# Stores of the routed experts' outputs: issued from GpSimd's queue instead of SyncE's

## What is computed

```python
logits = x @ router_w                                      # 8 experts, top 2 for each node
combine, dispatch = _top2_gating(logits, capacity)
expert_in = jnp.einsum('nec,nh->ech', dispatch, x)         # 196 slots for each expert
hmid = jax.nn.silu(jnp.einsum('ech,ehf->ecf', expert_in, w1) + b1[:, None, :])
expert_out = jnp.einsum('ecf,efh->ech', hmid, w2) + b2[:, None, :]
y = jnp.einsum('nec,ech->nh', combine, expert_out)
shared = jax.nn.silu(x @ sw1 + sb1) @ sw2 + sb2
out = y + SHARED_SCALE * shared
```

## Time and profile before

| | us |
|---|---|
| median of 3 runs | 1102.03 |
| lowest, highest | 1101.57, 1110.56 |
| profiled execution: its time | 1103.43 |
| profiled execution: span of the instructions | 1101.7 |
| routed experts, first turned slots to the last product of `own` | 973 to 1091 |

### The profile page before, as it was taken

How to read it: one execution, slowest core, us unless ns; L and a number is a source line. 1 busy time by engine, 2 the same in 40 slices (tenths; PEclk the granted TensorE clock), 3 DMA queues, 4 the chain that set the end, 5 groups by cost and what they waited for, 6 DMA issues and landing times.

```text
span 1101.7 us, 14500 instructions
## 1 busy us (share of the span) xinstructions
PE 1063.3 (97%) x5385; PEld 888.4 (81%) x5385; DVE 796.7 (72%) x1632; ACT 416.4 (38%) x647; POOL 410.9 (37%) x264
## 2 busy tenths in 40 slices
PE   6999999999999999999999998999979999999995
PEld 4888778778777777889999998877746877978874
DVE  7587779898989897228676766485479738866647
ACT  3432333443434333132323233451442515246752
POOL 4243788788888775042432230000010000310016
PEclk9999999999999999999999999999989999989997
DMA  9898776788887657687767542523242201578757
GB/s 334 315 316 246 168 209 106 182 229 210 204 228 158 163 121 175 76 187 182 194 169 184 133 123 99 210 93 117 66 73 86 83 2 43 226 264 299 253 184 259
DMA packets 91850, 191.92 MB, mean 174 GB/s; under 512 B 29722, under 2 KB 54877, under 8 KB 83323
## 3 DMA queue, kind: packets, MB, share of 16 engines
q1 hardware_dynamic: 38336, 126.11, 35.5%
q0 software_dynamic: 36032, 33.86, 16.8%
q10 hardware_dynamic: 17406, 30.97, 10.1%
HBM read 136.79 MB, written 54.11 MB: 173 GB/s over the span
## 4 chain that ended last, share of the span: by engine, by line
PE 87%; DVE 9%; ACT 2%; DMA 1%; issue 1%; ACTq 0%; POOLq 0%; SPq 0%; DVEq 0%
PE ps L588 69%; PE ps L896 5%; PE ps L933 4%; DVE rl L418 3%; PE ps L860 2%; DVE EQ L1583 1%; PE ps L578 1%; PE ps L911 1%; DVE V L1503 1%; PE ps L944 1%; PE ps L1027 1%; DMA stage<-in_w_rel 1%; PE ps L813 1%; ACT rh L409 1%; ACT He L1111 1%
## 5 line engine op out<-in xcount | busy, mean ns | idle before, releaser
L2225 POOL DMA_INDIRECT adj_scratch<-cnt,idx x164 | 287.0, 1750 | 131.8 <-DVE idx L1591 51.7
L418 DVE TENSOR_TENSOR rl<-stage,rh 128x512 fp32r<-128x512 f32 (+1 forms) x264 | 215.8, 845 | 138.8 <-ACT rh L409 135.3
L409 ACT CAST rh<-stage 128x512 fp32r<-128x512 f32 (+1 forms) x264 | 181.6, 714 | 343.1 <-PE ps L588 259.9
L588 PE MATMUL ps<-rh,xTh 128*125 128x512 f32 x600 | 237.6, 396 | 1.9 <-DVE xTl L1562 1.0
L588 PE MATMUL ps<-rh,xTl 128*125 128x512 f32 x600 | 236.2, 394 | 0.0
L588 PE MATMUL ps<-rl,xTh 128*125 128x512 f32 x600 | 236.1, 393 | 0.0
L588 PE MATMUL ps<-rh,Ar 125*125 125x342 f32 x600 | 190.8, 323 | 4.6 <-issue 3.3
L588 PE MATMUL ps<-rl,Ar 125*125 125x342 f32 x600 | 190.2, 322 | 0.0
L588 PEld LDWEIGHTS ps<-rh,xTh 128*125 128x125 f32 x600 | 111.1, 185 | 31.6 <-ACT He L1111 1.9
L588 PEld LDWEIGHTS ps<-rh,xTl 128*125 128x125 f32 x600 | 111.2, 185 | 28.0
L588 PEld LDWEIGHTS ps<-rl,xTh 128*125 128x125 f32 x600 | 111.2, 185 | 27.0
(11 more groups left out here) (296 smaller groups left out, 1616.8 us busy)
## 6 DMA issues: line engine op xcount, KB each, us to landing
stage<-in_w_rel SPq DMA_DIRECT2D x22, 1024.0 KB, 6.5
stage<-h_scratch SPq DMA_DIRECT2D x24, 855.0 KB, 6.6
stage<-in_w_e SPq DMA_DIRECT2D x16, 1024.0 KB, 5.3
h_scratch<-He ACTq DMA_DIRECT2D x40, 257.0 KB, 8.2
h_scratch<-He ACTq DMA_DIRECT2D x40, 256.0 KB, 4.2
KR<-key_scratch ACTq DMA_DIRECT2D x37, 256.0 KB, 5.1
stage<-in_w_gate SPq DMA_DIRECT2D x8, 1024.0 KB, 6.1
U<-xe_scratch POOLq DMA_DIRECT2D x16, 392.0 KB, 5.7
```

Source lines behind the costliest of these rows:

```text
L409: e.copy(h, s).then_inc(*a_hi.up(*[("hi", t) for t in step(i)]))
L418: e.tensor_tensor(l, s, h.bitcast(F32), ALU.subtract).then_inc(*v_lo.up(*[("lo", t) for t in step(i)]))
L588: ins = e.matmul(ps[0:P, b, 0:width], a, m, start=first and n == 0, stop=last and n == len(parts) - 1, skip_group_check=again)
L2225: e.indirect_dma_start(accd[to], bass.IndirectOffsetOnAxis(ap=idx[:, n:n + 1], axis=0), cnt16[:, n:n + 1], None, compute_op=ALU.add).then_ ...
```

## The change

The loop in SyncE's program no longer has the stores; it only loads the remaining weights, each as soon as its staging buffer is free. GpSimd's program has the stores instead, with the same two waits for each: after the loads of rows for experts 0 to 4 it alternates the stores of expert n with the loads of rows for expert n + 5, and then issues the rest of the stores. Size and number of all transfers stay, as do the semaphores that they count up.

```diff
-            for n in range(7):
-                for j in range(2):
-                    s, (_, row) = (2 * n + j) % 3, xe_row(n, j)
-                    for hf in range(2):
-                        on.wait_ge(*at("eo", n, j, hf))
-                    e.dma_start(eod[row:row + HC, :], EOs[:, s, :]).then_inc(*d_eo[s].up(("eo out", n, j)))
-                for g in range(first("s1", 0) + 9 + 2 * n, first("s1", 0) + 11 + 2 * n):
-                    if g < len(groups):
-                        load(g)
+            for g in range(first("s1", 0) + 9, len(groups)):
+                load(g)
...
-            for n in range(8):
+            def results_out(n):
+                for j in range(2):
+                    s, (_, row) = (2 * n + j) % 3, xe_row(n, j)
+                    for hf in range(2):
+                        on.wait_ge(*at("eo", n, j, hf))
+                    e.dma_start(eod[row:row + HC, :], EOs[:, s, :]).then_inc(*d_eo[s].up(("eo out", n, j)))
+
+            for n in range(5):
                 slots_in(n)
+            for n in range(7):
+                results_out(n)
+                if n + 5 < 8:
+                    slots_in(n + 5)
```

## The result

| | before | after |
|---|---|---|
| median of 20 runs each, us | 1106.77 | 1109.45 |
| lowest, highest | 1100.98, 1111.67 | 1104.88, 1117.43 |
| profiled execution: time | 1103.43 | 1114.99 |
| its span | 1101.7 | 1113.2 |

The ratio is 1.0044, with a 95% interval of 1.0029 to 1.0058: by the ratio the change costs 4.9 us (3.2 to 6.4), by the medians of the table 2.7. Forecast were +0.7 and 1102.7 us, in a range up to 1106. Part of the distance in absolute time isn't the change: the three runs ahead of the forecast had a median of 1102.03, twenty of the same kernel have 1106.77. In the kernel after, lines behind SyncE's changed loop are 7 lower than before (L926 is L933, L1374 is L1381), and in GpSimd's program L2316 and L2320 are the L2312 and L2316 of before.

What follows compares the result with a forecast made beforehand. Products were taken to bound the stage, and the last store's landing and the add chain the end. +0.22 us issue and +0.50 us packets gave +0.7, on the median 1102.03 making 1102.7 us; range 1101.0 to 1106.

Steps and rivals of the forecast that it cites:

- What bounds the kernel: Routed experts' stage: bound by TensorE's products, 12.50 us in 12.50 us, with the DMA engines 90% busy.
- SyncE's part: SyncE's queue loses 14 stores and 28 waits; staging buffers release the loads, so none starts earlier: value 0.
- at the same distances: Sign in the profile after: weight loads on SyncE still released by low parts, with unchanged distances.
- R1: Rival: stores fight weight loads; 2.7 us late costs nothing, beyond 3.6 us TensorE stalls, to 1111 us; chance 0.12.
- The mild form of R1: Weight loads just over the edge, TensorE stalling 1 us in two or three periods: 1105 us; within R1's chance 0.12.
- The last store: Expert 6's second store, issued by GpSimd: +0.22 us to issue, +0.50 us to first packets, sum +0.7 (+0.2 to +1.7).
- GpSimd's start after the eviction: Issue of the last store after its result's eviction: 0.29 us on GpSimd against SyncE's 0.07, so +0.22 us.
- The chain at the end: After 1064: gathers, sums and adds follow each other in order, each 0.7 us later; the end moves by all 0.7.
- R3: Rival: adds shifted over 1.2 us let VectorE's chunk 2 sum go first, giving back 1.2 us; chance 0.02.
- Copies waiting for stores: ScalarE's copy into a result buffer waits for the store three places before: hidden, or 0.4 us at a 5.3 us store.
- loads of rows behind results: GpSimd's loads of rows 5 to 7 behind waits for results of experts 0 to 2: over 4 us spare, value 0.
- R2: Rival: VectorE holds up GpSimd's writing of descriptors for the last store: +1.0 us more, 1103.7 us; chance 0.06.

Runs made afterwards that it cites:

- pool_double: Kernel after with each store of experts 0 to 4 issued twice from GpSimd, once into an unread tensor; ratio 1.0169, median 1124.78 us.
- sp_double: Kernel before with each store of experts 0 to 4 issued twice from SyncE, once into an unread tensor; ratio 1.0063, median 1113.75 us.
- again: The kernel after run once more, unchanged, against the kernel before; ratio 1.0036, median 1109.48 us.
- split kernels: Each expert weight load cut into two DMAs, applied to before (ratio 0.9995, 1104.97 us) and to after (1.0003, 1106.31 us).

## Why the prediction was wrong

**What bounds the kernel: wrong, though the rows were read right.** "The stage that the change touches is bound by products" held in the one profiled execution. In two others of the same kernel it was bound by the loop of weight loads for stretches. One profile could not show that.

**SyncE's part: right.** Loads are still released by low parts (VectorE's end at 1013.21 + 1.91 = 1015.12, the load at 1015.20), and none comes earlier for lack of stores ahead of it. My sign "at the same distances" did not hold: in after the loads of this buffer are 13.4 and 16.3 us apart (1001.81, 1015.20, 1031.48).

**R1, the slack: here is the step that failed.** I gave the stores against the weight loads 0.12 and set the edge at "3.6 us of room. So 2.7 us late costs nothing". I had followed a late landing once forward, to the slots' low parts and TensorE. That room exists, but as a reserve that is used up: lateness also goes backward, from the low parts to the next load's issue, and comes around again. The edge of a repeated lateness is the loop's, 7.1 us for a load. Before, the loads into this buffer issued at 1012.27 and 1024.50 took:

```profile
stage<-in_w_e SPq DMA_DIRECT2D x1, 1024.0 KB, 6.5
...
stage<-in_w_e SPq DMA_DIRECT2D x1, 1024.0 KB, 8.1
```

The second was already over the edge and the first had 0.6 us to it, not 3.6; and the reserve made up for it. All numbers for that were at hand: that load landed at 1024.50 + 8.1 = 1032.6, the next one into the buffer was issued at 1037.74, 5.1 us later, and 12.25 us is the period. The lateness was mis-sized as well. I added 2.7 us to a load of 5.5, which was one into the other buffer; the loads of the loop became 8.3, 11.2 and 9.9 us, up to 4.7 us more than the 6.5 of before. The mild form of R1, at 1105, was the right mechanism with too small a weight. What the gaps cost through the clock, most of 3.6 us in after, stood in none of my sums.

The Trainium skill, DMA: Bandwidth & Descriptors, "Queues, rings and completion order", says that each DMA engine takes turns between the queues that have work. The 11.7 us between `pool_double` and `sp_double`, with the same bytes, agree with it; that a load in line is served ahead of the stores behind it is my reading and not shown, since I didn't follow single packets. The Trainium skill, DMA: Bandwidth & Descriptors, "Issuing engine by pattern", which sends simple stores to SyncE, was right in its direction. The 0.4 us of first byte, by which I had weighed it, is the smaller part of the loss.

**The last store: right, at the upper side.** +0.7 was forecast (+0.2 to +1.7); +1.05, +1.06 and +0.4 us were measured against the 5.14 us of before. The mis-sized term is GpSimd's start after the eviction: 0.53 us in place of 0.29, so +0.46 and not +0.22. Between the split kernels, 6.23 against 4.24 us, it was +2.0.

**The chain at the end: right in the main.** The chain of after runs through the gathers and an add, no longer through L1027. The first gather is 10.9 us later and the end 11.5: the issue of the ten gathers took 14.7 us in after and 13.7 before, for which I had no term. R3, the changed order, did occur in one profile: in after the first two adds are 2.6 us apart, since VectorE's sum had gone first. From the last gather's issue to the end of the span it is 17.7 us, before 18.1; the other two profiles of before have 19.0 and 19.3, so what R3 gave back can't be told from that.

**Copies waiting for stores, loads of rows behind results: nearly right.** No wait of ScalarE for a store and none of TensorE for rows appears in after's stage. In `again` the last copy waited 0.57 us for a store, the case that I had priced at 0.4. R2 did not occur at the last store; its row was also thinner than I wrote, since the gather at 1076.59 took only 0.95 us beside the sum of 1076.71.

**The size.** +1 us of the 4 to 5 was forecast with its mechanism; +3 to +4 was a rival that I had priced out.

## What to carry to other kernels

Room in a pipeline with few buffers is the period minus everything in one turn of a buffer (landing to release, release to landing), not the distance from a late landing to the engine that matters; compare it with the slowest load seen, not the usual one. Where transfers fill the DMA engines to 90%, as here, it matters in whose queue they stand: the doubled stores cost 11.7 us less in the queue of the urgent loads than in one of their own. A gap of TensorE can cost more than its length, when a stretch at the lower clock follows. And before a stage is called bound by an engine, look at a second profile: one execution without stalls proves none.

## What the runs showed of the hardware

A store of 98 rows from GpSimd starts 0.53 to 0.59 us after the copy it waits for, from SyncE 0.07. From the last eviction to the first gather it was 5.6 to 6.2 us with GpSimd's store, 4.2 to 5.1 with SyncE's and 4.9 with ScalarE's. One 1 MB load took between 6.8 and 12.5 us in the same place of the same kernel. With two half stores in place of the last whole one, the first gather came 0.6 us nearer (4.24 us, 3.64). After gaps of TensorE the granted clock was 0.74 in the window 1040 to 1053 of after, where it was 1.00 without gaps before. What makes the DMA system slow in some executions already near 970, before any store of results, stays open; it lies in the kernel before as well.
